# Softmax attention: 49-row stacks in two 64-row tiles, four stack buffers, maximum scores in pairs

## The reference

```python
q, k, v = split(layernorm(x) @ w_attn)          # 16 heads of 16 columns
attn = einsum('bhqd,bhkd->bhqk', q, k) * 0.25   # T = 1024 queries and keys
attn = where(causal, attn, -inf)
out  = einsum('bhqk,bhkd->bhqd', softmax(attn), v)
```

## Time and profile before

| | |
|---|---|
| runs | 4138.56 us median, 4131.36 to 4143.86 |
| profiled execution | span 4136.6 us; the page tells of no time outside it |
| busy share of the span | TensorE 82%, VectorE 58%, ScalarE 36%, GpSimd 20% |
| the phase that is changed | from about 240 us (its first memset) to about 1416 us |
| L493 reduces of the maximum scores | 743.5 us in 1248 |
| L523 exponentials | 597.7 us in 768 |
| L551 and L578 score matmuls | 470.3 and 466.9 us, 1536 each |
| L594 products | 330.1 us in 3072, up to four at once |
| L554 masks of the maximum scores | 188.9 us in 736 |

### The profile page before, as it was taken

The page is one execution under the profiler, slowest core; times in us unless marked ns, Lnnn a source line. Parts: engine busy times, 40 slices in busy tenths (PEclk is TensorE's granted clock), DMA queues, the critical chain, the costliest instruction groups (busy, mean ns, idle before and its releaser), DMA issues. The chain is left out here.

```text
span 4136.6 us, 62031 instructions
## 1 busy us (share of the span) xinstructions
PE 3388.8 (82%) x21377; PEld 2546.4 (62%) x21377; DVE 2384.2 (58%) x5007; ACT 1507.4 (36%) x2286; POOL 839.8 (20%) x1006
## 2 busy tenths in 40 slices
PE   6859999999999766579564776999566599999998
PEld 5735555555555465569343564777466488888887
DVE  5546666666666377683123785555477644444544
ACT  2315555555555433334002662000133323333333
POOL 0021111111111122234674663000122100000000
PEclk9879999999999878789656998999777699999999
DMA  6884666666666256563565996666344433233331
GB/s 191 234 146 60 85 85 85 85 81 84 84 85 84 74 184 200 183 214 127 132 139 138 345 346 217 210 207 206 108 153 153 158 84 85 86 81 81 81 81 51
DMA packets 452026, 570.37 MB, mean 138 GB/s; under 512 B 94544, under 2 KB 300400, under 8 KB 450672
## 3 DMA queue, kind: packets, MB, share of 16 engines
q1 hardware_dynamic: 440064, 544.45, 52.3%
q0 software_dynamic: 10240, 14.16, 2.0%
q10 hardware_dynamic: 1648, 10.81, 0.7%
HBM read 329.62 MB, written 238.61 MB: 137 GB/s over the span
## 5 line engine op out<-in xcount | busy, mean ns | idle before, releaser
L493 DVE TENSOR_REDUCE att_mx<-att_m_ps 128x1 f32<-128x512 f32 (+4 forms) x1248 | 743.5, 645 | 381.6 <-PE att_m_ps L554 324.1
L523 ACT ACTIVATE att_pr<-att_e_ps 128x1024 f32<-128x1024 f32 (+3 forms) x768 | 597.7, 811 | 366.5 <-PE att_e_ps L578 362.3
L551 PE MATMUL att_m_ps<-att_ks,att_qs 128*128 128x512 f32 (+3 forms) x1536 | 470.3, 377 | 99.5 <-PEq L39 95.4
L578 PE MATMUL att_e_ps<-att_qs,att_ks 128*128 128x512 f32 (+3 forms) x1536 | 466.9, 386 | 10.5 <-PEq L39 9.0
L475 POOL TENSOR_SCALAR_AFFINE_SELECT att_pr<-att_pr 128x256 f32<-128x256 f32 x512 | 206.7, 407 | 938.5 <-PEq L571 931.9
L578 PEld LDWEIGHTS att_e_ps<-att_qs,att_ks 128*128 128x128 f32 x1536 | 249.1, 194 | 239.9 <-issue 186.7
L551 PEld LDWEIGHTS att_m_ps<-att_ks,att_qs 128*128 128x128 f32 x1536 | 280.0, 195 | 155.2 <-issue 93.7
L594 PE MATMUL att_o_ps<-att_pr,att_vs 128*17 128x512 f32 (+3 forms) x3072 | 330.1, 502 | 0.0
L2116 DVE TENSOR_TENSOR ffn_hid<-ffn_gate,ffn_u_ps 128x512 f32<-128x512 f32 x192 | 132.1, 688 | 249.5 <-PE ffn_u_ps L698 213.1
L2164 ACT ACTIVATE ffn_hh<-ffn_hid 128x512 fp32r<-128x512 f32 x192 | 121.4, 633 | 421.5 <-DVE ffn_hid L2120 319.3
L698 PE MATMUL ffn_y_ps<-ffn_wld,ffn_hh 128*128 128x256 f32 x768 | 216.9, 282 | 0.0
(11 more groups left out here) (286 smaller groups left out, 8168.2 us busy)
## 6 DMA issues: line engine op xcount, KB each, us to landing
prj_o<-attended SPq DMA_DIRECT2D x32, 1024.0 KB, 5.0
ffn_wt<-weights SPq DMA_DIRECT2D x16, 2048.0 KB, 16.0
att_qs<-q_high SPq DMA_DIRECT2D x64, 256.0 KB, 5.8
att_qs<-q_low SPq DMA_DIRECT2D x64, 256.0 KB, 8.7
att_ks<-k_high SPq DMA_DIRECT2D x64, 256.0 KB, 12.3
att_ks<-k_low SPq DMA_DIRECT2D x64, 256.0 KB, 15.9
attended<-att_ot SPq DMA_DIRECT2D x64, 256.0 KB, 2.2
prj_x<-x SPq DMA_DIRECT2D x32, 512.0 KB, 5.9
```

What stands on the lines that cost most here:

```text
L493: e.reduce_max(mx[:, h, heads[0]:heads[-1] + 1, q], src, AX.X).then_inc(m_free, 1)
L523: e.activation(pr[:, u % NPR, 2 * p:2 * p + 2, 0:w], e_ps[:, s % 2, :, 0:w], ACT.Exp).then_inc(exp_done, 1)
L551: ins = e.matmul(out[:, i], qs[:, j, hd, q * P:(q + 1) * P], ks[:, j, hd, h * BLK:h * BLK + w], start=i == 0, stop=h != q // 4, skip_group ...
L578: i = e.matmul(e_ps[:, s % 2, n, 0:w], ks[:, j, hd, k * P:(k + 1) * P], qs[:, j, hd, (h + 1) * BLK - w:(h + 1) * BLK], start=True, stop=True)
```

## The change

The stack loses its fourth part (ql.kl) and has 48 rows, with the row of maxima behind them 49. Heads 0 and 1 of a group lie in partitions 0 to 48, heads 2 and 3 in 64 to 112. Each matmul of scores then covers at most 49 rows from partition 0 or 64, and two of them, one in each half, follow each other directly, into two PSUM banks. The maximum scores leave the row of maxima out (48 rows). There are four stack buffers; the load is for the group three ahead. A load is twelve DMAs of 128 KB and the values; the row of maxima is two DMAs; the zeros are gone, since the row beyond the maxima isn't read.

Units of 256 and 128 columns take all four heads in one step: 20 steps. The pieces become 21 pairs, 42 pieces. In a masked pair the two causal matmuls come first, then the scores. Products of a unit now stand ahead of the unit's scores, for the unit 3 back (LAG). In a step the exp scores are written first, then one pair is computed; pairs left over follow the last step of the unit. The pairs of the group after the next begin at unit TURN = 8.

```diff
-    NBUF = 3
+    NBUF = 4
+    LAG = 3
+    HALF, MAXROW = P // 2, 3 * HD
-        qs = ph.sb("qs", [P, NBUF, GH, T], f32r)
+        qs = ph.sb("qs", [P, NBUF, 2, T], f32r)
 ...
+        for u, (h, k) in enumerate(units):
+            steps += [(u, (0, 1))] if width(h, k) <= BLK // 2 else [(u, (0,)), (u, (1,))]
 ...
+        whole, partial = [], []
+        for q in range(KB):
+            for h in range(q // 4 + 1):
+                both = 2 * keys(q, h) <= BLK and q != 1
+                (partial if h == q // 4 else whole).extend((q, h, ps) for ps in (((0, 1),) if both else ((0,), (1,))))
+        pairs, taken = [], 0
+        for n, piece in enumerate(partial):
+            pairs.append(piece)
+            while taken < len(whole) and taken + 1 <= len(whole) * (n + 1) / len(partial):
+                pairs.append(whole[taken])
+                taken += 1
+        TURN, MAXIMA = 8, 16
 ...
                 def load(g, j):
+                    for n in range(2):
+                        for dst, parts in ((qs, ("qh", "qh", "ql")), (ks, ("kh", "kl", "kh"))):
+                            for r, name in enumerate(parts):
+                                at = n * HALF + r * HD
+                                e.dma_start(dst[at:at + HD, j].bitcast(fp32), src_rows[name][g][:, 2 * n:2 * n + 2]
+                                            ).then_inc(stack_loaded[j], 16)
                     e.dma_start(vs[:, j], v_rows[g]).then_inc(stack_loaded[j], 16)
-                    e.dma_start(maxima_row(j), zero[:]).then_inc(stack_loaded[j], 16)
 ...
                     if loads:
-                        load(g + 2, (nxt + 1) % NBUF)
+                        load(g + 3, (nxt + 2) % NBUF)
 ...
-                e.wait_ge(consts, NBUF)
-                e.wait_ge(first_here, 1)
+                e.wait_ge(later_ones, 2)
                 for j in range(1, NBUF):
                     load(j, j)
 ...
+                def maxima_pair(j, i):
+                    q, h, ps = pairs[i]
+                    w, masks = keys(q, h), h == q // 4
 ...
+                    for n in range(2):
+                        if masks:
+                            e.wait_ge(m_free, 2 * i + n + 1)
+                            e.matmul(out[n][:, :, w - P:w], identb[:],
+                                     causal[:].unsqueeze(1).broadcast_to((P, len(ps), P)), start=True, stop=False,
+                                     skip_group_check=True)
+                    for m, p in enumerate(ps):
+                        for n in range(2):
+                            if not masks and m == 0:
+                                e.wait_ge(m_free, 2 * i + n + 1)
+                            rows = slice(n * HALF, n * HALF + MAXROW)
+                            ins = e.matmul(out[n][:, m], qs[rows, j, p, q * P:(q + 1) * P],
+                                           ks[rows, j, p, h * BLK:h * BLK + w], start=not masks and m == 0,
+                                           stop=m == len(ps) - 1, skip_group_check=True)
+                            if m == len(ps) - 1:
+                                ins.then_inc(m_scores, 1)
 ...
                 def scores(j, s):
-                    for n in range(2):
-                        hd = 2 * p + n
-                        i = e.matmul(e_ps[:, s % 2, n, 0:w], ks[:, j, hd, k * P:(k + 1) * P],
-                                     qs[:, j, hd, (h + 1) * BLK - w:(h + 1) * BLK], start=True, stop=True)
+                    for m, p in enumerate(ps):
+                        for n in range(2):
+                            rows = slice(n * HALF, n * HALF + MAXROW + 1)
+                            i = e.matmul(e_ps[:, s % 2, n, m * w:(m + 1) * w], ks[rows, j, p, k * P:(k + 1) * P],
+                                         qs[rows, j, p, (h + 1) * BLK - w:(h + 1) * BLK], start=m == 0,
+                                         stop=m == len(ps) - 1, skip_group_check=True)
 ...
                 def group(j, first, more, more2):
+                    for u in range(UNITS):
+                        if not (first and u < LAG):
+                            products(j, u - LAG)
+                        if u == TURN and more2:
+                            e.wait_ge(stack_loaded[nxt2], LOADS)
+                            take(e, (stack_loaded[nxt2], LOADS))
+                        due = list(share[u]) if (more2 if u >= TURN else more) else []
+                        for s in of_unit[u]:
+                            exponentials(s, first)
+                            if s == MAXIMA and more:
+                                maxima()
+                            scores(j, s)
+                            for i in due[:1]:
+                                maxima_pair(nxt2 if u >= TURN else nxt, i)
+                            due = due[1:]
+                        for i in due:
+                            maxima_pair(nxt2 if u >= TURN else nxt, i)
```

More of the change, by code:

```diff
@@ L338, in phase_softmax_attention @@
         ot_stored = [ph.sem(f"ot_stored{j}") for j in range(2)]
-        LOADS = 16 * 10
+        LOADS = 16 * 13
+        ROWS = 16 * 2
         LOOPS = (G - 4) // NBUF
[L343 to L357, removed]
+        assert 1 + LOOPS * NBUF + 3 == G
         def width(h, k):
@@ L363, in keys @@
             return min(BLK, (q + 1) * P - h * BLK)
+        units = [(h, k) for h in range(2) for k in range(4 * h + 4)]
+        UNITS = len(units)
+        steps = []
+        for u, (h, k) in enumerate(units):
+            steps += [(u, (0, 1))] if width(h, k) <= BLK // 2 else [(u, (0,)), (u, (1,))]
+        NS = len(steps)
+        of_unit = [[s for s in range(NS) if steps[s][0] == u] for u in range(UNITS)]
         def diagonal(s):
-            h, k, p = steps[s]
+            h, k = units[steps[s][0]]
@@ L367, in diagonal, with masks_before @@
             return k * P >= h * BLK
+        NDIAG = sum(diagonal(s) for s in range(NS))
+        def masks_before(u):
+            return sum(diagonal(s) for v in range(-LAG, u + 1) for s in of_unit[v % UNITS])
+        whole, partial = [], []
[4 more added lines that the diff above has]
+        pairs, taken = [], 0
@@ L369, in shares @@
+        for n, piece in enumerate(partial):
[3 more added lines that the diff above has]
+                taken += 1
+        NPAIR, NPC = len(pairs), 2 * len(pairs)
+        TURN, MAXIMA = 8, 16
+        assert NPC % MBUF == 0 and taken == len(whole) and width(*units[steps[MAXIMA][0]]) <= BLK - P
+        assert MAXIMA % 2 == 0 and steps[MAXIMA][0] > TURN
         def shares():
-            order = list(range(MEND, len(steps))) + list(range(MEND))
@@ L372, in shares @@
-            load = [keys(q, h) * len(heads) + 96 for q, h, heads in pieces]
-            work = [width(*steps[s][:2]) + 160 for s in order]
+            order = list(range(TURN, UNITS)) + list(range(TURN))
+            load = [keys(q, h) * len(ps) + 64 for q, h, ps in pairs]
+            work = [sum(width(*units[u]) * 2 * len(steps[s][1]) + 80 for s in of_unit[u]) for u in order]
             out, n, done, due = {}, 0, 0.0, 0.0
-            for s, w in zip(order, work):
+            for u, w in zip(order, work):
@@ L376, in shares @@
                 due += w * sum(load) / sum(work)
-                out[s] = []
-                while n < NPC and done + load[n] / 2 <= due:
+                out[u] = []
+                while n < NPAIR and done + load[n] / 2 <= due:
                     done += load[n]
-                    out[s].append(n)
+                    out[u].append(n)
                     n += 1
+            assert n == NPAIR
             return out
         share = shares()
-        NDIAG = sum(diagonal(s) for s in range(len(steps)))
@@ L386, in phase_softmax_attention @@
[L386 to L390, removed]
         src_rows = {n: d.rearrange("(g h d) t -> g d h t", h=GH, d=HD)
@@ L514, in group @@
                 def group(first, more):
-                    for s, (h, k, p) in enumerate(steps):
-                        w, u = width(h, k), s // 2
+                    for s, (u, ps) in enumerate(steps):
+                        w = width(*units[u])
                         if s == MAXIMA and more:
```

143 lines of the change are left out of this document (57 added, 86 removed).

## The result

The changed kernel takes 4423.91 us (median of four runs, 4411.04 to 4497.77; the highest was a disturbed run and is not in the ratio) against 4140.42: ratio 1.0679, 95% interval 1.0657 to 1.0701. The profiled run took 4423.42 us. The forecast was 3974, its range 3910 to 4095.

A forecast was written before the change was run, and what follows sets the result against it. TensorE was taken to set the pace. A group falls from 35.0 to 28.9 + 0.8 = 29.7 us, 31 x 5.3 = 164 less; with 1 at the ends, 4136.6 - 165 = 3972, as a median 3974; range 3910 to 4095.

The forecast's parts named there:

- rival D: In the groups: the maxima row 3 to 4 us late, or the clock falling; period about 32, 4045 us; chance 0.10.
- forecast 2.4: TensorE's waits for VectorE: the larger engine's work in each of 12 units, 28.9 us a group against 26.5 of TensorE work.
- 0.8 for the copy of `o_ps`: Start of units 3 and 7: products wait for the copy behind unit 2's exp; TensorE 0.8 us late a group in all.
- A: Score pairs: the two weight loads run in turn; 32.4 us a group, 4057 us; chance 0.22.
- C: Each of 48 score pairs: row tiles don't overlap, 17.7 us in place of 8.9; 4203 us; chance 0.12.
- E: Score pairs: each runs as two full-array matmuls, no overlap and no tile changes; 34.1 us a group, 4110 us; chance 0.03.
- 26.5 forecast: TensorE's work in one group: pairs, blocks, tile changes, bare loads, causals and transposition sum to 26.5 us, against 31.2.
- 0.09 for each change of tile: TensorE entering or leaving tiles: 0.09 us each, 50 changes a group, 4.6 us.
- rival B: Masked pairs: row tiles change with the full array at no cost; TensorE 22.7, period 28.4 us, 3933 us; chance 0.13.
- the wait for the stack: TensorE's wait for the third stack, 2.0 us a group, goes with four buffers.
- the row of maxima never late: Row issued near 24 us into the group, landing at 26 to 28, needed at 29.6: hidden, under 3 us to spare.
- forecast 305 for the first exp scores: Prologue: the first row of maxima stands behind four loads, so the start is at 305, about 1 us later.

The follow-up runs named there:

- experiment 2: The kernel before the change, with its score matmuls over rows 0 to 64 of the stack instead of all 128: 4632.3 us.
- kernel 1: The changed kernel with every score matmul over all 64 rows of its half, the added rows being zero: 4199.70 us, ratio 1.0118.
- experiment 10: Here its fastest version, e12: e8 with TensorE's loop over the groups written out, four buffers: 4004.21 us, ratio 0.9665.
- e5: The changed kernel with the row tiles alone undone, each score matmul over all 128 rows: 4168.69 us, ratio 1.0085.
- e8: kernel 1 with pairs of maximum scores never in direct succession, two places per unit with products between: 4040.04 us, ratio 0.9770.
- e12: e8 with TensorE's loop over the groups written out, so that it has no branch: 4004.21 us, ratio 0.9665.

## Why the prediction was wrong

**The clock (rival D, chance 0.10): the step that failed.** I had the earlier trace rows with a clock of 0.57 for 4 us, priced such a stretch at 2 us, and took "the third buffer and 26 us of work in 30" as the reason against it. Work in 30 is busy time, and experiment 2 shows TensorE busy 99% at 0.55. What the change takes away is rows: 128 became 98, and nothing in the sum had a term for that. That waits for VectorE can start such a stretch was right; its length of 4 us didn't carry over, since in the changed kernel waits of 0.3 to 0.4 us stand before stretches of 14 to 126 us. The lost clock costs about 10.7 of the 44.5 us of a group (44.5 less 32.9 of work and waits at full clock, taken from kernel 1, less 0.9 for the branch), 31 times: some 330 us.

**VectorE (forecast 2.4, and 0.8 for the copy of `o_ps`): mis-sized.** Measured about 6.7 a group in kernel 1, nearly all behind pairs in direct succession, and none for `o_ps`: of the seven waits at L618 (14.0 us), six stand right behind a branch of the loop and one in the last group. I took the larger of two sums in each unit of the written order, as if one engine could run ahead of the other inside a unit. With three banks and two taken per pair it can't. These are 3.5 us too few, 109 in all, and the order that makes them is the one that loses the clock.

**The loop's branch: not foreseen.** It adds 3.5 us to every fourth group, 0.9 in the mean, 21 us in six passes. The rows of before have it at 0.2 us.

**Right:** two row tiles in the time of one (rivals A, C and E fell: pairs 0.23 apart, not 0.47, and their weight loads together); the work of TensorE, 26.5 forecast and 26.2 measured, with 0.09 for each change of tile in it (rival B, 22.7, fell too); the wait for the stack gone; the row of maxima never late. The Trainium skill (TensorE: Matmul & The Clock Gate, Part 3) has row tiles starting about 4 ns after one another; the two matmuls of a pair are mostly 1 to 5 ns apart here, so the trace agrees.

**The head:** forecast 305 for the first exp scores, measured 297.43. The row of maxima was issued at 289.17 and in by 297.4, so the loads ahead of it took less than I had given them: 7.6 us in the kernel's favour.

By terms: forecast 29.7; 3.5 more of waits and 0.3 less of work, as kernel 1 has them: 32.9; branch 0.9; clock 10.7: 44.5. With the clock held and the pairs spread, the same row tiles give 31.0 (experiment 10), and the sum of work would have allowed 26.2; the 4.8 between are what VectorE still takes. It is busy 705.8 of 920 us there, 23.8 of the 31.0.

Two small slips in the sum change nothing: by its own rows the twelve blocks come to 8.15 us and not 8.0 (36 times 0.213 and 12 times 0.04), and today's reduces to 23.2 a group (743.5 over 32) and not 23.6.

Left open: how rows and pauses combine to one clock (the table has twelve points and no rule), and what exactly makes the 34.8 us of the full array in the new order (e5); its sum of 31.5 and 3.6 of waits for VectorE would account for it, an estimate that no run isolates.

## What to carry to other kernels

Read TensorE's granted clock beside its busy share, and before narrowing a contraction or packing it in row tiles, ask how many rows the array will span: fewer rows can halve the clock of everything on TensorE, the untouched products too, and a short pause is then paid for much longer. Padding with zero rows up to the full tile costs no matmul time and was worth 5% here. When work comes in pairs for three PSUM banks, put other work between two pairs. Try the parts of a change alone: the three-part stack by itself gave 2.1%.

## What the runs showed that I had not expected

- The falls of the clock stand behind pauses, and the rows decide how long a fall lasts: behind the wait for the stack under 4 us with 128 rows, up to 413 us of unbroken work with 65.
- Rows of zeros hold the clock. The same kernel with 128, 96 and 65 rows fed, the rest being zeros: clock 0.98, 0.94, 0.59 and 4139, 4177, 4632 us.
- TensorE's branch back to a loop of four groups took 3.3 to 3.8 us, with three groups 0.2. With the loop written out the period went from 32.15 to 30.97 (e8, e12), with no longer group left.
- Two weight loads of one pair of row tiles overlap. The timeline of weight loads of the changed kernel has two in the time of one:

```profile
702.36 0.19 PEld L601 LDWEIGHTS att_e_ps<-att_qs,att_ks 49*128 49x128 f32 x2
```
